# Lane 0's Newton squares on all four quadrants of TensorE, with image 1 copied back across partitions, in a vision transformer block

## The reference

```python
kernel_1 = softmax(einsum(q, keys_landmarks))       # 64 landmarks = 64 tokens here
kernel_2 = softmax(einsum(queries_landmarks, keys_landmarks))
kernel_3 = softmax(einsum(queries_landmarks, k))
V = 1.0 / denom * swapaxes(K, -1, -2)               # K = kernel_2
for _ in range(6):
    KV = matmul(K, V)
    V = matmul(0.25 * V, 13 * I - matmul(KV, 15 * I - matmul(KV, 7 * I - KV)))
out = matmul(matmul(kernel_1, V), matmul(kernel_3, v))
```

## Time and profile before

| what | value |
|---|---|
| median of 3 runs | 736.73 us (735.62 to 738.35) |
| the profiled execution | 739.34 us, its span 737.6 us |
| PE busy | 680.3 us, 92% of the span |
| PEld busy | 595.5 us, 81% |
| DVE busy | 496.5 us, 67% |
| ACT busy | 356.3 us, 48% |
| POOL busy | 108.2 us, 15% |
| chain that ended last | PE 76%, DVE 14%, ACT 5%, issue 3% |
| share of L364 in that chain | 24% of the span |
| `qq` copies L557 | 192 of 128x384, 490 ns each |

### The profile page before, as it was taken

How to read it: one execution, slowest core, us unless ns; L and a number is a source line. 1 busy time by engine, 2 the same in 40 slices (tenths; PEclk the granted TensorE clock), 3 DMA queues, 4 the chain that set the end, 5 groups by cost and what they waited for, 6 DMA issues and landing times.

```text
span 737.6 us, 30455 instructions
## 1 busy us (share of the span) xinstructions
PE 680.3 (92%) x13218; PEld 595.5 (81%) x13218; DVE 496.5 (67%) x1354; ACT 356.3 (48%) x921; POOL 108.2 (15%) x328
## 2 busy tenths in 40 slices
PE   5668999999999999999999999869999999999996
PEld 2457888788888888888888878748898898998986
DVE  5257778777878878877778877447456546646644
ACT  0125664655655655555555655534334344434432
POOL 0122123123123123223123211110000000000000
PEclk9969999999999999999999999979999999999999
DMA  8951111011011011111000000000000000000000
GB/s 311 300 182 60 61 48 44 33 44 48 33 60 33 32 60 32 32 61 32 32 4 5 4 4 4 4 1 2 1 1 21 0 0 21 0 0 21 0 0 22
DMA packets 12244, 30.48 MB, mean 41 GB/s; under 512 B 1120, under 2 KB 7392, under 8 KB 11616
## 3 DMA queue, kind: packets, MB, share of 16 engines
q1 hardware_dynamic: 12128, 28.73, 11.9%
HBM read 27.16 MB, written 1.57 MB: 39 GB/s over the span
## 4 chain that ended last, share of the span: by engine, by line
PE 76%; DVE 14%; ACT 5%; issue 3%; DMA 1%; POOL 1%; DVEq 0%; ACTq 0%; SPq 0%; POOLq 0%
PE ps L364 24%; PE ps L493 17%; PE ps L484 15%; PE ps L263 6%; DVE uu L734 3%; DVE sq L653 2%; PE ps L277 2%; PE ps L382 2%; PE ps L314 2%; DVE rf L741 2%; ACT qq L557 2%; PE ps L448 2%; PE ps L278 1%; ACT rr L561 1%; PE ps L375 1%
## 5 line engine op out<-in xcount | busy, mean ns | idle before, releaser
L884 DVE SCALAR_TENSOR_TENSOR acc<-ps,comb,acc 128x192 f32 x256 | 89.2, 411 | 90.3 <-PE ps L493 90.3
L493 PE MATMUL ps<-w_sb,work 128*128 128x192 f32 x768 | 139.9, 326 | 0.5 <-ACT work L633 0.3
L364 PE MATMUL ps<-rr 64*64 64x64 f32 x3840 | 131.4, 221 | 6.0 <-issue 3.3
L493 PEld LDWEIGHTS ps<-w_sb,work 128*128 128x128 f32 x768 | 129.2, 189 | 9.5 <-issue 1.7
L364 PEld LDWEIGHTS ps<-rr 64*64 64x64 f32 x3840 | 119.8, 136 | 18.7 <-ACT rr L561 10.6
L557 ACT ACTIVATE qq<-ps 128x384 f32<-128x384 f32 x192 | 92.3, 490 | 66.7 <-PE ps L364 64.7
L734 DVE SCALAR_TENSOR_TENSOR uu<-rr,qq 128x384 f32<-128x384 f32 x160 | 87.9, 559 | 50.8 <-ACT qq L557 44.6
L633 ACT ACTIVATE work<-ps 128x512 f32<-128x512 f32 x96 | 57.3, 597 | 133.6 <-PE ps L484 133.6
L561 ACT ACTIVATE rr<-ps 128x384 f32<-128x384 f32 x160 | 73.9, 490 | 80.6 <-PE ps L364 79.8
L364 PE MATMUL ps<-uu,qq 64*64 64x64 f32 x4608 | 96.6, 224 | 16.1 <-DVE uu L734 13.9
L364 PEld LDWEIGHTS ps<-uu,qq 64*64 64x64 f32 x4608 | 80.6, 134 | 33.9 <-DVE uu L734 30.6
(11 more groups left out here) (136 smaller groups left out, 1026.8 us busy)
## 6 DMA issues: line engine op xcount, KB each, us to landing
xtb<-xt_dram SPq DMA_DIRECT2D x16, 512.0 KB, 3.5
work<-x_dram SPq DMA_DIRECT2D x16, 512.0 KB, 3.4
wsh<-ws_dram SPq DMA_DIRECT2D x2, 1440.0 KB, 7.8
w_sb<-w_dram SPq DMA_DIRECT2D x1, 2304.0 KB, 26.3
w_a<-w_dram SPq DMA_DIRECT2D x1, 1536.0 KB, 13.2
w_b<-w_dram SPq DMA_DIRECT2D x2, 768.0 KB, 17.7
out_dram<-acc SPq DMA_DIRECT2D x4, 384.0 KB, 2.7
mult<-copies_dram SPq DMA_DIRECT2D x1, 512.0 KB, 12.8
```

The lines of the kernel that those rows point to most:

```text
L364: last = pe.matmul(ps[z:z + 64, 2 * lane + i, 64 * j:64 * j + 64], lhs[r, lane, i, j, :], rhs[r, lane, i, j, :], start=True, stop=True)
L493: last = pe.matmul(ps[:, 2 + 2 * (e % 2) + j // 2, (j % 2) * DIM:(j % 2 + 1) * DIM], hid[:, c % 4, j * P:(j + 1) * P], w2_sb[:, c, :], sta ...
L884: last = dve.scalar_tensor_tensor(out=a, in0=ps[:, 2 + 2 * (e % 2) + j // 2, (j % 2) * DIM:(j % 2 + 1) * DIM].unsqueeze(1), scalar=comb[:, ...
```

## The change

Lane 0's squares of image 1 now write to the other half of the partitions, so lane 0's squares use all four quadrants; lane 1's stay on two. Since `qq` has to lie as `rr` does, ScalarE copies lane 0 in three pieces: image 0 (128 partitions x 192 columns), then image 1 from PSUM partitions 64 to 127 into SBUF partitions 0 to 63, and from 0 to 63 into 64 to 127 (64 x 192 each). `q_ready` now counts four per step, and VectorE waits for three of them for lane 0 and for the fourth for lane 1.

```diff
@@ pe newton
-                            z = 64 * (half ^ (i * phase))
+                            crossed = i == 1 and (phase == 1 or lane == 0)
+                            z = 64 * (half ^ crossed)
@@ act newton
-                    act.activation(qq[:, lane].rearrange("p i h n -> p i (h n)"), ps[:, 2 * lane:2 * lane + 2, 0:LC],
-                                   ACT.Copy).then_inc(q_ready, 1)
+                    q = qq[:, lane].rearrange("p i h n -> p i (h n)")
+                    if lane == 0:
+                        act.activation(q[:, 0], ps[:, 0, 0:LC], ACT.Copy).then_inc(q_ready, 1)
+                        for a in (0, 64):
+                            act.activation(q[a:a + 64, 1], ps[64 - a:128 - a, 1, 0:LC], ACT.Copy).then_inc(q_ready, 1)
+                    else:
+                        act.activation(q, ps[:, 2:4, 0:LC], ACT.Copy).then_inc(q_ready, 1)
@@ dve newton_sum
-                dve.wait_ge(q_ready, n + 1)
+                dve.wait_ge(q_ready, 4 * (STEPS * t + k) + 3 + lane)
```

## The result

The change makes the kernel a little slower: 739.06 us median (737.38 to 742.03, 13 runs) against 736.96 (735.34 to 738.81, 13 runs) of before; the ratio is 1.0035, with a 95% interval of 1.0024 to 1.0047. Forecast were 731.0 us and a range of 721.5 to 737.0.

The account below looks back on a forecast made before the run. TensorE looked like the bound (26.14 of 27 us busy), though the chain differed by step. Gains of 0.39 us an iteration over tiles 0 to 12 plus 0.2 for each of the last three made 5.7 us: 731.0 us, range 721.5 to 737.

Parts of the forecast that it names:

- T = 0.97: Time from lane 0's first copy piece until lane 0 is whole: 0.97 us, each piece starting when the previous ends.
- step 3: Squares in the chain; lane 0's copies end 0.11 us before lane 1's old copy start: gain of 0.11 us an iteration.
- step 4: Squares off the chain; only lane 1's sum moves up behind lane 0's: gain of 0.10 us an iteration.
- step 1: ScalarE and VectorE nearly as long as TensorE, 0.2 us slack; later copies and sums lose 0.50 us an iteration.
- step 5: Products start when TensorE's qk matmuls end, copies and sum being done earlier: gain of 0.34 us an iteration.
- Step 2: Pure TensorE in the chain, lane 0's copies and sum hidden: gain of 0.34 us an iteration.
- step 0: From `rf` to the products, one row of VectorE work that covers the copies: effect 0.
- (d): Rival: lane 0's squares on four quadrants still take 0.74 us, only the losses stay; 748 us, chance 0.04.
- (b): Rival: copy pieces stand alone with gaps, T 1.01, lane 1 at 1.04; gain 0.15 us an iteration, 734.5 us, chance 0.20.
- The last tiles: Last three tiles lack `tok`, so TensorE bounds fewer steps: half the gain, 0.2 us each.
- (e): Rival: TensorE's longer wait lowers its clock, in every iteration 27 us; a few per cent, 0.06 with the like.
- (c): Rival: copies crossing partitions run long, T = 1.31, from 0.38 us a piece; loss 0.62 us an iteration, 746.6 us, chance 0.10.

Follow-up runs that it names:

- the shared kernel: Change in steps 2, 3 and 5 of tiles 0 to 13, VectorE copying half of image 1 in step 3, against before: 726.77 us, ratio 0.9873.

## Why the prediction was wrong

What failed is the step on the copies' overlap, T = 0.97, and behind it the gains of 0.11 and 0.10 for steps 3 and 4: T measured 1.01, and those steps lost 0.07 and 0.05. By step, the forecast of -0.39 us an iteration missed the measured +0.10 by 0.49: 0.18 in step 3, 0.15 in step 4, 0.08 in step 1, and the rest in step 5 and behind `rf`.

- **The bound by step.** Right for steps 0, 1, 2 and 5. Step 2 and step 5 are TensorE's and gained 0.35 and 0.29; step 1 is ScalarE's and VectorE's and lost; step 0 isn't touched. The part that was misleading is to call TensorE the bound from its 26.14 of 27 us.
- **TensorE's saving, 0.34 us.** Right: 0.35. Rival (d) falls. The Gram rows had rightly shown that a tile times itself can be fast.
- **The pieces' durations.** Near: 0.332 and 0.316 forecast; 0.329 and 0.325 measured.
- **Their overlap, T = 0.97.** This is the step at which the forecast left the truth: "each starts when the one before ends". Measured are gaps, T 1.01 and lane 1's start at 1.03, which is rival (b) to 0.01 us. I had read the gap off and still summed with the value between, for which the prediction gives no reason. The experiments show that a change of source or of destination is each enough. Step 1 then lost 0.58, as (b) has it (0.57). In the prediction's own terms T = 1.01 turns the gain of 0.39 into 0.15, which is 0.24 of the 0.49.
- **Steps 3 and 4.** The larger part of the miss, 0.33 of the 0.49, and wrong under (b) too: they lost 0.12 us, where (b) had a gain of 0.04. In step 3 I took the sums as 0.56 each. The change's own lane 0 sum there took 0.70, since it too ran into GpSimd's residual (234.44 to 235.04); its row stands below. The pair ended 2.88 us after the squares' start, 2.75 before, and 0.10 of that 0.13 is the longer pair (1.17 against 1.07 in step 2). I had named GpSimd nowhere. In step 4 the prediction has no term for lane 0's copies: it lets the sums begin where VectorE's row ends. But ScalarE has `x2t` and `xhi` first, and the chain now runs through them and all three pieces (237.04 to 238.63). VectorE's own row ends at 238.60, so this costs the start only what the two no longer overlap; the first sum begins 1.72 us after the squares' start instead of 1.59.

```profile
234.76 0.70 DVE L740 SCALAR_TENSOR_TENSOR uu<-rr,qq 128x384 f32<-128x384 f32 x1 [0.83 <-ACT qq L562]
```

- **The last tiles.** The term furthest off for its size: I gave them half of the gain, 0.2 each, without a reading of their windows. The last two lost 2.6 us in the profiled execution, some 2.0 without its gap and its clock fall. In those tiles the three copies cost more than the faster squares save. With them (b)'s small gain becomes a small loss, and the run without them shows it.
- **Rival (e), the clock.** Not as priced: the iterations of the change run at 1.00, and the mean granted clock is 0.981 in both profiled executions. But a small share is open. Between the first and the last `rf` each execution has one stretch of 3.4 us at 0.50: before in tile 10, 2.9 us behind a TensorE gap of 0.49 at 347.73; in the change in tile 15, after 3.4 us in which it was busy for 2.29. The prediction's "It fell once" holds only for that part of the span, since the clock is also low near 40 and 50 us, near 485 and at the end. Over the runs, the change's 13 average 0.978, and the longest (742.03, 740.62 and 740.25 us) have the lowest, 0.972 or 0.973; later sets of runs of the kernel before average 0.981, and there a mean lower by 0.01 goes with 2 to 4 us. By this estimate up to 1 us of the 2.1 can be the clock's; no run separates it.

```profile
351.10:354.50 3.40, 3.40 (x52) 3.28 (x52) 1.63 (x5) 2.30 (x6) 0.00 (x0) 0.50 0.30 110
```

```profile
472.20:475.60 3.40, 2.29 (x86) 1.98 (x86) 1.25 (x3) 2.29 (x6) 0.72 (x1) 1.00 0.02 5
475.60:479.00 3.40, 2.94 (x91) 2.75 (x82) 1.12 (x2) 2.43 (x9) 0.00 (x0) 0.51 0.02 5
```

- The prices of (c) and (d) count the last three tiles in full, where the forecast counts them half; counted alike, (c) is 745.7 and not 746.6. Nothing hangs on it.
- The chances gave 0.20 to (b), "can't be told from no change", and the result lies within 0.5%, but 2.1 us beyond the range: its upper end stood on (b) with a gain, and (c), which I priced, needs copies of 0.38. Errors of the same sign in three small terms were not in it.

What stays open: the few iterations in any one execution that are longer, by some tenths of a us up to 4.5. They are not spread at random. In the fifteen traces TensorE has 57 gaps of over 0.2 us between the first and the last `rf` that no dependency explains; all of them stand in step 4, 51 in its squares, and only in tiles 2 to 4, 8 to 10, 13 and 14. The longest iterations, 30.07 to 31.27 us, have the granted clock at 0.50 for 6.8 us as well. No run was made on the cause. Open is also why a change of the first partition takes the overlap away on ScalarE; the runs show that it does for source and for destination.

## What to carry to other kernels

Price a change in a software pipeline step by step, and once more for the tiles at the ends, whose windows are partly empty: there the added latency of the copies cost more than the faster squares gave. When a faster engine hands work to one that copies it out, make the change only at the steps that the faster engine bounds: the same edit at steps 2 and 5 alone is worth 0.8%, at step 1 it costs 1.3%. And when a step's gain doesn't arrive, look for one instruction whose duration grew, and at what ran on GpSimd at that moment.

## What the runs showed of the hardware

- ScalarE copies that start at the same partition overlap by 0.10 to 0.13 us; where source or destination starts in the other half, there is none, and a gap of 0.02 to 0.03 us. For a piece of 0.33 us that is 0.35 instead of 0.23.
- Copying from one half of the partitions to the other costs nothing extra: a 64x192 piece averages 0.325 us crossed and takes 0.31 to 0.33 straight.
- A 128x384 sum of two SBUF tensors on VectorE took 0.98 us instead of 0.56 when it began 0.04 us after a 128x192 sum of two SBUF tensors on GpSimd. Begun 0.04 to 0.34 us after it, such a sum ended 0.41 or 0.42 us after the GpSimd one's end, 96 times in eight traces; GpSimd's kept its 0.60 (in the shared kernel, 255.95 to 256.55). A margin of 0.06 us was all that kept them apart before.
- 48 weight loads of 64x64 that use two quadrants take 1.48 us, four quadrants 0.79 to 0.81, also where both operands are one tile (0.79 in the run with both lanes crossed).
- At a granted clock of 0.50 instead of 1.00, 48 matmuls of 64x64 on four quadrants took 1.57 us instead of 1.09.
